# Two slots of their own for the gate inputs that are loaded back, and their first two loads ahead of the last two stores

## The chip, the cores and the metric

The kernel runs on one core of a Trainium2 chip. The metric is the device time of one execution in microseconds (us); with several runs it is their median. Times inside an execution are counted from the start of its profiled span.

## The reference, cut to what matters

Two layers follow each other, both with a residual sum: a graph layer (a gather of rows, scaled and summed by destination) and an LSTM whose hidden states are mixed into running sums.

```
support = layernorm(x) @ W.T + b                       # 6250 x 256
x = x + segment_sum(support[dst] * edge_weight, src)   # 100000 edges
z = layernorm(x)
xp = z @ W_ih.T + b_ih + b_hh                          # gate inputs, 6250 x 1024
for t in range(6250):                                  # one sequence
    i, f, g, o = split(xp[t] + h @ W_hh.T)
    c = sigmoid(f) * c + sigmoid(i) * tanh(g)
    h = sigmoid(o) * tanh(c)
w = argmax(h @ W_lin.T + b_lin) * h
out = x + 2 * h + prefix(w) * fw + suffix(w) * bw
```

## The kernel before, in words

The sequence of 6250 rows is cut into 125 segments of 50 rows. All segments are run side by side, as the 125 columns of one step. Each segment starts 64 steps early, so that its state has settled when its own rows begin: steps 0 to 63 run over rows that lie ahead of the segment, steps 64 to 113 over its own. The gate input of one row of every segment is one block of 128 partitions by 1016 values (508 KB). Each block is used two or three times.

The program has three long stages. First the edges are sorted into buckets, and the first portion of them is gathered and summed. In the second stage (about 755 to 1505 us) the edges of one row of every segment, a "place", are gathered in 12 tiles. GpSimd issues one indirect DMA for each tile (L522), TensorE multiplies the tile by a weighted one-hot matrix (L1539), and VectorE adds the product (L1046). Three places later the row is finished: it is normalised, projected to the gate input (L1558), and step u of the LSTM (L1565) runs straight from it. So steps 0 to 49 run beside the gather. The last place is 49, and step 49 runs after the last tile. In the third stage, from about 1518 us on, steps 50 to 113 run with no gather; their gate inputs are loaded back from HBM.

`take_input` (ScalarE, L640) writes the gate input of place j into slot q = j mod 2 of the tile `pr`. `seed_half` (L648) copies half of a slot into a PSUM bank as the start of the gate sums, and counts `seeded[x]`. `store_gate_input` (SyncE, L400) waits for `xe_r[1]`, stores the slot to `gate_input_scratch` and counts `st2[q]`. `load_gate_input` (L413) loads a block back into the same slot q of `pr` and counts `xp_l[q]`. ScalarE waits for that in `seed_loaded`, whose waits also hold the seed until the step before has read the bank.

Each engine works through its own instructions in order. SyncE issues the stores and the loads. A load into `pr` may go out only when the store that reads the same slot has landed and when the seeds that read it are done. In the program before, the order at the end of the second stage is store 48, load 50, store 49, load 51, and then a loop of loads from 52 on. On ScalarE the order is the rest of step 49 (its last operation is a tanh, L669), the two seeds of step 50, the two seeds of step 51, and then step 50. Step 50 on TensorE needs both seeds of step 50 and the hidden state of step 49.

Of the kernel before, what the change touches and what calls it, by code (L numbers as in the profile page):

```python
# [6 lines left out]
P = 128  # L7
# [5 lines left out]
SEGS, SEGL = 125, 50  # L13
# [28 lines left out]
LEAD = WARM - SEGL  # L42
LAG = 3
XW = SEGS + 2
XC = 8 * XW
# [12 lines left out]
def build(nc, A, out, slow_sweeps=SEGS, tol=TOL):  # L58
# [6 lines left out]
    ds = bass.ds  # L65
# [4 lines left out]
    xp_d = nc.dram_tensor("gate_input_scratch", [SEGL, P, XC], f32).ap()  # L70

    with ExitStack() as ctx:
        def sb(name, shape, dt=f32):
            return ctx.enter_context(nc.sbuf_tensor(name, shape, dt))
# [4 lines left out]
        def sem(name):  # L79
            return ctx.enter_context(nc.semaphore(name))  # L80
# [51 lines left out]
        pr = sb("pr", [P, 2, G4])  # L132
# [7 lines left out]
        flat_c = big_c[:].rearrange("p b f -> p (b f)")  # L140
# [3 lines left out]
        def at(home, first, rows, *dims, dt=f32):  # L144
            size = 1
            for n in dims:
                size *= n
            words = -(-size // 2) if dt == bf16 else size
            view = home[0:rows, first:first + words]
            if dt != f32:  # L150
                view = view.bitcast(dt)[:, 0:size]
            names = "abcde"[:len(dims)]
            spaced = " ".join(names)
            return view.rearrange(f"p ({spaced}) -> p {spaced}", **dict(zip(names, dims))) if len(dims) > 1 else view
# [58 lines left out]
        weighed = (w_even, w_odd)  # L213
        own = big_a[0:SEGS, :, :]
        x1 = big_b[0:SEGS, :, :]
        gate_in = [pr[:, q, 0:XC].rearrange("p (c k) -> p c k", c=8) for q in range(2)]


# [66 lines left out]
        st2 = [sem(f"gate_input_stored{i}") for i in range(2)]  # L285
        xp_l = [sem(f"gate_input_loaded{i}") for i in range(2)]
        bits = sem("gate_banks_written_once")
        small_t = sem("bias_and_logit_columns_in_psum")
        seeded = [sem(f"gates_seeded{x}") for x in range(2)]
# [48 lines left out]
        def _(sp):  # L338
# [35 lines left out]
            for g in range(-(-NB // STORED)):  # L374
                first, n = g * STORED, min(STORED, NB - g * STORED)
# [21 lines left out]
            def store_gate_input(j, l, q):  # L397
                sp.wait_ge(xe_r[1], j + 1)
                row = l if isinstance(l, int) else sp.snap(l)
                sp.dma_start(xp_d[ds(row, 1), :, :].rearrange("o p n -> p (o n)"), pr[:, q, 0:XC]).then_inc(st2[q], 16)  # L400
# [6 lines left out]
                    store_gate_input(it * 2 + q, it * 2 + (q - LEAD), q)  # L407

            def load_gate_input(u, l, q):
                for x in range(2):  # L410
                    sp.wait_ge(seeded[x], u - 1)
                row = l if isinstance(l, int) else sp.snap(l)
                sp.dma_start(pr[:, q, 0:XC], xp_d[ds(row, 1), :, :].rearrange("o p n -> p (o n)")).then_inc(xp_l[q], 16)  # L413

            for q in range(2):
                store_gate_input(SEGL - 2 + q, SEGL - 2 + q - LEAD, q)
                sp.wait_ge(st2[q], 16 * (SEGL // 2))
                load_gate_input(SEGL + q, SEGL - LEAD + q, q)
            with sp.Fori(SEGL // 2 + 1, WARM // 2) as it:
                for q in range(2):  # L420
                    load_gate_input(it * 2 + q, it * 2 + (q - LEAD), q)
            with sp.Fori(WARM // 2, STEPS // 2) as it:
                for q in range(2):
                    load_gate_input(it * 2 + q, it * 2 + (q - WARM), q)
# [139 lines left out]
        def _(act):  # L564
# [69 lines left out]
            def take_input(j, q, x, free=None):  # L634
                act.wait_ge(pj2[x], j + 1)
                if free is not None:
                    act.wait_ge(seeded[x], free)
                    act.wait_ge(st2[q], j * 8 - q * 8)
                for c in range(4):
                    ins = nc.scalar.activation(gate_in[q][:, 4 * x + c, 2:XW], bank[2 + x][:, c * SEGS:(c + 1) * SEGS],  # L640
                                               ACT.Identity, bias=bias[:, 4 * x + c:4 * x + c + 1])
                ins.then_inc(xe_r[x], 1)
# [1 line left out]
            def copy_input(j, q, first=False):  # L644
                copy_transposed(j, q, xt_p2, pj2[1], xt_r2, first, 2)

            def seed_half(q, x, w, b):
                nc.scalar.copy(bank[b + x][:, 0:4 * SEGS].rearrange("p (c k) -> p c k", c=4),  # L648
                               gate_in[q][:, 4 * x:4 * x + 4, w:w + SEGS]).then_inc(seeded[x], 1)

            def seed_loaded(u, pair, q, w, used=-1):
                act.wait_ge(xp_l[q], pair * 16 - (SEGL // 2 * 16 - 16))
                for x in range(2):
                    act.wait_ge(a_o[x], u + used)
                for x in range(2):
                    seed_half(q, x, w, 2 * q)

            def gates(u, q, x, far, b=None):
                g = bank[(2 * q if b is None else b) + x]
# [17 lines left out]
            def take_and_seed(u, q, w):  # L677
                for x in range(2):
                    take_input(u, q, x, None if isinstance(u, int) and u < 2 else u - 1)
                    act.wait_ge(xe_r[x], u + 1)  # L680
                    if not isinstance(u, int) or u > 0:
                        act.wait_ge(a_o[x], u)
                    seed_half(q, x, w, 0)

            def place(it, q, w=0, last=False):
                h = 2 * it + q if isinstance(it, int) else HALVES
                j, u = it * 2 + (q - LAG), it * 2 + (q - LAG - 1)
                if h > LAG + 1:
                    tanh_c(u - 1, 1 - q, 1)
                if h > 0 and not last:  # L690
                    act.wait_ge(prod, it * WIDE + (RING + TFROM[1] + q * PACE))
                    stage_gather(it * WIDE + (TFROM[1] + (q + 1) * PACE), 1 - q, PACE)
                if h > LAG:
                    take_and_seed(u, q, w)
                    for x in range(2):
                        gates(u, q, x, False, 0)
                    tanh_c(u, q, 0)
                if h >= LAG:
                    copy_input(j, 1 - q, h < LAG + 2)
# [16 lines left out]
            place(HALVES // 2, 0, 1, True)  # L716
            tanh_c(SEGL - 2, 0, 1)
            take_and_seed(SEGL - 1, 1, 1)
            step(SEGL - 1, 1, False, 0)
            seed_loaded(SEGL, SEGL // 2, 0, 1, 0)  # L720
            act.wait_ge(bits, 2)
            seed_loaded(SEGL + 1, SEGL // 2, 1, 1)
            with act.Fori(SEGL // 2, (WARM - 2) // 2) as it:
                for q in range(2):
                    step(it * 2 + q, q)
                    seed_loaded(it * 2 + (q + 2), it + 1, q, 1)
# [11 lines left out]
            with act.If(ok == 0):  # L738
# [6 lines left out]
                with act.Fori(0, slow_sweeps) as sweep:  # L745
# [4 lines left out]
                    with act.Fori(0, SEGL // 2 - 1) as it:  # L750
                        u, m = sweep * SEGL + it * 2 + STEPS, sweep * (SEGL // 2) + it + STEPS // 2
# [1004 lines left out]
```

## Time and profile before

| | us |
|---|---|
| median of three runs | 1850.2 |
| the three runs | 1849.69, 1850.2, 1853.89 |
| the profiled execution | 1853.58 |
| its span | 1851.8 |
| mean granted TensorE clock | 0.885 of full |
| TensorE busy | 1388.0 (75%) |
| VectorE busy | 1365.8 (74%) |
| GpSimd busy | 1204.2 (65%) |
| ScalarE busy | 543.2 (29%) |

The span lies between the first and the last instruction of the profiled execution; 1.8 us of its time lie around the span. The busy shares are averages over stages that have different limits, so they say little about a change at one point. What counts is what each engine waits for between about 1457 and 1523 us, where the last gathers, the last two stores and the first loads follow each other.

### The profile page before, as it was taken

What the parts mean: (1) busy time and instruction counts of PE and PEld (TensorE: products, weight loads), DVE (VectorE), ACT (ScalarE), POOL (GpSimd) and SP (SyncE); (2) the same over time, 40 slices, a digit from 0 to 9 for tenths busy, and PEclk for the clock granted to TensorE, in tenths of its full rate; (3) what the DMA queues carried; (4) which work ended last, traced back from release to release, by engine and by line L of the source; (5) the groups of instructions that cost most, each with busy time, mean ns of one, the idle gap of its engine ahead of it and who ended that gap; (6) DMA issues with size and microseconds to landing.
All of it is one profiled execution on the core that took longest, in us unless ns stands there. A gap on an engine that the chain in (4) does not pass through costs nothing.

```text
span 1851.8 us, 34357 instructions
## 1 busy us (share of the span) xinstructions
PE 1388.0 (75%) x8625; PEld 1154.8 (62%) x8625; DVE 1365.8 (74%) x4146; ACT 543.2 (29%) x1869; POOL 1204.2 (65%) x1275
## 2 busy tenths in 40 slices
PE   5587744554555458998988888889889878999991
PEld 2345533443444333787777777777777668899991
DVE  7979778888888955677777777777777644566665
ACT  1112200000000000333333333333333346666660
POOL 0304867777777757777777777777777700477772
PEclk9778967777777775899999999999999999999995
DMA  8101343333333643444444444444444763333334
GB/s 210 26 23 35 50 137 76 79 79 74 80 79 74 77 61 106 128 137 141 144 138 138 139 137 139 139 136 139 138 137 137 109 124 114 113 113 112 113 101 139
DMA packets 77430, 202.26 MB, mean 109 GB/s; under 512 B 28529, under 2 KB 30790, under 8 KB 76392
## 3 DMA queue, kind: packets, MB, share of 16 engines
q0 software_dynamic: 53808, 116.85, 27.3%
q1 hardware_dynamic: 23584, 84.98, 14.2%
q8 instruction: 15, 0.25, 0.1%
q14 instruction: 23, 0.19, 0.0%
HBM read 160.49 MB, written 41.10 MB: 109 GB/s over the span
## 4 chain that ended last, share of the span: by engine, by line
PE 27%; POOL 24%; DVE 22%; issue 17%; DVEq 3%; DMA 3%; ACT 3%; SPq 0%; POOLq 0%; ACTq 0%
POOL big_a L522 22%; PE bank L1565 10%; DVE big_a L975 7%; PE bank L1485 5%; PE bank L1539 5%; PE bank L1514 4%; PE bank L1558 1%; DVEq L1049 1%; DVE big_c L1166 1%; ACT big_c L669 1%; DVE big_c L1171 1%; DVE listed L914 1%; ACT bank L662 1%; DVE stats L893 1%; PE bank L1433 1%
## 5 line engine op out<-in xcount | busy, mean ns | idle before, releaser
L522 POOL DMA_INDIRECT big_a<-support_scratch,stg_g x636 | 608.3, 956 | 207.0 <-issue 192.3
L1539 PE MATMUL bank<-big_a,big_c 128*125 128x256 f32 x1272 | 412.3, 416 | 92.0 <-issue 51.0
L1565 PE MATMUL bank<-big_c 128*128 128x125 f32 x3648 | 457.2, 277 | 26.9 <-DVE big_c L1171 23.8
L1565 PEld LDWEIGHTS bank<-big_c 128*128 128x128 f32 x3648 | 446.7, 192 | 48.7 <-issue 36.0
L1046 DVE TENSOR_TENSOR big_b<-big_b,bank 125x256 f32 x881 | 366.5, 416 | 132.0 <-PE bank L1539 82.9
L1040 DVE TENSOR_SCALAR big_c<-consts_sb,listed 128x125 f32<-128x125 f32 x881 | 318.8, 362 | 73.4 <-PE bank L1539 62.1
L1539 PEld LDWEIGHTS bank<-big_a,big_c 128*125 128x125 f32 x1272 | 202.7, 197 | 179.2 <-DVE big_c L1040 113.1
L492 POOL DMA_INDIRECT big_a<-support_scratch,stg_g x245 | 236.2, 964 | 82.2 <-issue 69.2
L1485 PE MATMUL bank<-big_a 125*128 125x192 bf16 x800 | 119.5, 332 | 214.1 <-DVE big_a L975 214.1
L1485 PEld LDWEIGHTS bank<-big_a 125*128 125x128 bf16 x800 | 100.4, 132 | 237.5 <-DVE big_a L975 229.4
L1558 PEld LDWEIGHTS bank<-xt,w_ih 128*128 128x128 f32 x1600 | 213.3, 195 | 13.8 <-ACT xt L578 1.9
L1558 PE MATMUL bank<-xt,w_ih 128*128 128x125 f32 x1600 | 214.0, 278 | 1.7 <-ACT xt L578 1.7
L604 ACT CAST stg_g<-listed 128x12 uint32 (+4 forms) x84 | 15.8, 190 | 472.4 <-PE bank L1514 387.4
L669 ACT ACTIVATE big_c<-big_c 128x125 f32<-128x125 f32 x228 | 70.4, 309 | 233.5 <-DVE big_c L1166 233.5
L1514 PE MATMUL bank<-big_a,big_c 128*125 128x256 f32 x490 | 129.0, 414 | 11.6 <-DMA big_a<-support_scratch,stg_g 9.1
L640 ACT ACTIVATE pr<-bank,gate_bias 128x125 f32<-128x125 f32 x400 | 113.3, 367 | 75.1 <-PE bank L1558 74.4
L537 POOL TENSOR_TENSOR listed<-listed 125x256 f32<-125x256 f32 x50 | 36.5, 729 | 142.7 <-DVE listed L1295 142.5
L648 ACT COPY bank<-pr 128x500 f32<-128x500 f32 x228 | 126.6, 573 | 3.2
L975 DVE TENSOR_TENSOR big_a<-big_a,bank 125x3840 bf16<-125x3840 bf16 x30 | 124.3, 4142 | 0.0
L662 ACT ACTIVATE big_c<-bank 128x250 f32<-128x250 f32 x128 | 48.3, 378 | 241.7 <-PE bank L1565 241.7
L1514 PEld LDWEIGHTS bank<-big_a,big_c 128*125 128x125 f32 x490 | 94.6, 208 | 37.0 <-issue 12.9
L463 POOL DMA_INDIRECT record_scratch<-stg_r,stg_i x60 | 95.6, 1593 | 21.5 <-issue 16.8
(226 smaller groups left out, 1658.4 us busy)
## 6 DMA issues: line engine op xcount, KB each, us to landing
pr<-gate_input_scratch SPq DMA_DIRECT2D x64, 508.0 KB, 3.4
gate_input_scratch<-pr SPq DMA_DIRECT2D x50, 508.0 KB
big_a<-support_scratch,stg_g POOLq DMA_INDIRECT x881, 2.8
out<-big_a SPq DMA_DIRECT2D x5, 1120.0 KB
support_scratch<-pr SPq DMA_DIRECT2D x12, 448.0 KB
big_b<-in_x SPq DMA_DIRECT2D x2, 1904.0 KB
big_b<-in_x SPq DMA_DIRECT2D x1, 1792.0 KB
w_ih<-in_w_ih SPq DMA_DIRECT2D x1, 1024.0 KB
```

The source lines that it names most:

```text
L492: pool.indirect_dma_start(out=ring[:, s, :], out_offset=None, in_=sup_d, in_offset=bass.IndirectOffsetOnAxis(ap=stg_g[:, q, j:j + 1], axis ...
L522: pool.indirect_dma_start(out=ring[:, s, :], out_offset=None, in_=sup_d, in_offset=bass.IndirectOffsetOnAxis(ap=stg_g[:, q, n:n + 1], axis ...
L640: ins = nc.scalar.activation(gate_in[q][:, 4 * x + c, 2:XW], bank[2 + x][:, c * SEGS:(c + 1) * SEGS], ACT.Identity, bias=bias[:, 4 * x + c ...
L648: nc.scalar.copy(bank[b + x][:, 0:4 * SEGS].rearrange("p (c k) -> p c k", c=4), gate_in[q][:, 4 * x:4 * x + 4, w:w + SEGS]).then_inc(seede ...
L975: V.tensor_tensor(col_v[:, q].rearrange("p c k n e -> p (c k n e)"), col_h[:, q].rearrange("p c (o n) e -> p c o (n e)", o=1).broadcast_to ...
L1040: V.tensor_scalar(oneh[:, s % HOTS, 0:SEGS], iota[:, 0:SEGS], src_of[:, ds(t, 1)], w_of[:, ds(t, 1)], ALU.is_equal, ALU.mult).then_inc(oh_ ...
L1046: V.tensor_tensor(at, at, bank[4 + s % PSR][0:SEGS, 0:D], ALU.add).then_inc(added, 1)
L1485: ins = mm(bank[q][:, 0:6 * NPOS], slot_h[:, q, c // 2, :, c % 2], col_v[:, q, c // 2, :, :, c % 2].rearrange("p k n -> p (k n)"), start=c ...
L1514: mm(bank[4 + s % PSR][0:SEGS, 0:D], oneh[:, s % HOTS, 0:SEGS], ring[:, s % RING, :], start=True, stop=True).then_inc(prod, 1)
L1539: mm(bank[4 + s % PSR][0:SEGS, 0:D], oneh[:, s % HOTS, 0:SEGS], ring[:, s, :], start=True, stop=True).then_inc(prod, 1)
L1558: ins = mm(bank[2 + x][:, c * SEGS:(c + 1) * SEGS], w_ih[:, k, g:g + P], xt[:, q, k, 0:SEGS], start=k == 0, stop=k == 1)
L1565: return mm(bank[b + x][:, c * SEGS:(c + 1) * SEGS], w_hh[:, k, g:g + P], h_s[:, q, k, :], start=False, stop=True, skip_group_check=True)
```

## The change

There are two edits. First, the blocks that are loaded back no longer go into `pr`. They go into two slots of their own, `taken_in`, a part of the tile `big_c` that is free by then, and the seeds of steps 50 to 113 read them there. Second, SyncE's order at the end of the second stage is now load 50, load 51, store 48, store 49. The first two loads no longer wait for the seeds, since nothing has been in the new slots before. Load 50 waits for store 46 and load 51 for store 47. A wait for the stores 48 and 49 stands ahead of the loop of loads.

```
+        taken_in = [at(flat_c, 8192 + 1024 * q, P, 8, XW) for q in range(2)]
...
             def load_gate_input(u, l, q):
-                for x in range(2):
-                    sp.wait_ge(seeded[x], u - 1)
+                if not isinstance(u, int) or u >= SEGL + 2:
+                    for x in range(2):
+                        sp.wait_ge(seeded[x], u - 1)
                 row = l if isinstance(l, int) else sp.snap(l)
-                sp.dma_start(pr[:, q, 0:XC], xp_d[ds(row, 1), :, :].rearrange("o p n -> p (o n)")).then_inc(xp_l[q], 16)
-
+                sp.dma_start(taken_in[q].rearrange("p c k -> p (c k)"), xp_d[ds(row, 1), :, :].rearrange("o p n -> p (o n)")).then_inc(xp_l[q], 16)
+
+            for q in range(2):
+                sp.wait_ge(st2[q], 16 * (SEGL // 2 - 1))
+                load_gate_input(SEGL + q, SEGL - LEAD + q, q)
             for q in range(2):
                 store_gate_input(SEGL - 2 + q, SEGL - 2 + q - LEAD, q)
+            for q in range(2):
                 sp.wait_ge(st2[q], 16 * (SEGL // 2))
-                load_gate_input(SEGL + q, SEGL - LEAD + q, q)
...
-            def seed_half(q, x, w, b):
+            def seed_half(q, x, w, b, home):
                 nc.scalar.copy(bank[b + x][:, 0:4 * SEGS].rearrange("p (c k) -> p c k", c=4),
-                               gate_in[q][:, 4 * x:4 * x + 4, w:w + SEGS]).then_inc(seeded[x], 1)
+                               home[q][:, 4 * x:4 * x + 4, w:w + SEGS]).then_inc(seeded[x], 1)
...
-                    seed_half(q, x, w, 2 * q)
+                    seed_half(q, x, w, 2 * q, taken_in)
...
-                    seed_half(q, x, w, 0)
+                    seed_half(q, x, w, 0, gate_in)
```

On SyncE, this is the program before at the end of the second stage. The first two rows are the end of the loop that stores places 14 to 47; `gate_input_ready1` is `xe_r[1]`, `gate_input_stored0` is `st2[0]`.

```order
L405 REGISTER_ALU
L405 COMPARE_AND_BRANCH
L400 DMA gate_input_scratch<-pr 128x1016 [waits gate_input_ready1]
L413 DMA pr<-gate_input_scratch 128x1016 [waits gates_seeded1,gates_seeded0,gate_input_stored0]
L400 DMA gate_input_scratch<-pr 128x1016 [waits gate_input_ready1]
L413 DMA pr<-gate_input_scratch 128x1016 [waits gates_seeded1,gates_seeded0,gate_input_stored1]
L419 UNCONDITIONAL_BRANCH
```

The same place in the changed program:

```order
L406 REGISTER_ALU
L406 COMPARE_AND_BRANCH
L415 DMA big_c<-gate_input_scratch 128x1016 [waits gate_input_stored0]
L415 DMA big_c<-gate_input_scratch 128x1016 [waits gate_input_stored1]
L401 DMA gate_input_scratch<-pr 128x1016 [waits gate_input_ready1] x2
L424 UNCONDITIONAL_BRANCH [waits gate_input_stored1,gate_input_stored0]
```

The two loads stand right behind store 47, the last one of the loop, and the two last stores stand behind both loads.

On ScalarE, this is the end of step 49 and what follows it in the program before (`c_ready1` is the new cell state of the second half).

```order
L669 ACTIVATE big_c<-big_c 128x125 [waits c_ready1]
L648 COPY bank<-pr 128x500 [waits act_o_done1,act_o_done0,gate_input_loaded0]
L648 COPY bank<-pr 128x500
L648 COPY bank<-pr 128x500 [waits act_o_done0,act_o_done1,gate_input_loaded1,gate_banks_written_once]
L648 COPY bank<-pr 128x500
```

In the changed program:

```order
L674 ACTIVATE big_c<-big_c 128x125 [waits c_ready1]
L653 COPY bank<-big_c 128x500 [waits act_o_done1,act_o_done0,gate_input_loaded0]
L653 COPY bank<-big_c 128x500
L653 COPY bank<-big_c 128x500 [waits act_o_done0,act_o_done1,gate_input_loaded1,gate_banks_written_once]
L653 COPY bank<-big_c 128x500
```

Only the tile that the seeds read has another name; no instruction of ScalarE has moved, and none of TensorE, VectorE and GpSimd has.

## Rows read from the trace of the kernel before

**Rows 1.** The chain of waits from 1505 to 1524 us: start, length, what.

```profile
1506.09 3.85 PE bank L1558 x32
...
1511.12 2.66 DMA gate_input_scratch<-pr
1513.78 0.01 issue
1513.80 3.55 DMA pr<-gate_input_scratch
1517.35 0.03 ACTq L654
1517.38 0.51 ACT bank L648
1517.89 0.59 issue
1518.48 2.48 PE bank L1565 x20
```

**Rows 2.** Instructions of ScalarE in order of time, 1513 to 1519.6 us: start, length, what.

```profile
1517.09 0.31 ACT L669 ACTIVATE big_c<-big_c 128x125 f32<-128x125 f32 x1 [0.55 <-DVE big_c L1166]
1517.31 2.09 ACT L648 COPY bank<-pr 128x500 f32<-128x500 f32 x4
```

**Rows 3.** All engines in order of time, 1518 to 1545 us: step 51.

```profile
1520.98 0.38 ACT L662 ACTIVATE big_c<-bank 128x250 f32<-128x250 f32 x1 [1.58 <-PE bank L1565]
...
1523.69 0.31 ACT L669 ACTIVATE big_c<-big_c 128x125 f32<-128x125 f32 x1 [0.55 <-DVE big_c L1166]
1523.91 1.07 ACT L648 COPY bank<-pr 128x500 f32<-128x500 f32 x2
...
1525.57 0.38 ACT L662 ACTIVATE big_c<-bank 128x250 f32<-128x250 f32 x1 [0.59 <-PE bank L1565]
```

**Rows 4.** All engines, 1490 to 1518 us: SyncE's DMA issues.

```profile
1497.63 0.34 SPq L400 DMA_DIRECT2D gate_input_scratch<-pr  x1
...
1505.88 0.35 SPq L413 DMA_DIRECT2D pr<-gate_input_scratch  x1
```

**Rows 5.** SyncE alone, 1455 to 1480 us: the issue of store 47.

```profile
1475.19 0.33 SPq L400 DMA_DIRECT2D gate_input_scratch<-pr  x1
```

**Rows 6.** Busy time by stretch: stretch, its length, then PE, PEld, DVE, ACT, POOL, granted clock, DMA share, GB/s.

```profile
1420.00:1440.00 20.00, 18.09 (x122) 15.69 (x121) 14.64 (x66) 8.51 (x28) 15.13 (x17) 1.00 0.47 137
...
1460.00:1475.00 15.00, 11.79 (x60) 9.24 (x60) 8.19 (x33) 4.53 (x16) 11.36 (x12) 0.90 0.96 74
...
1485.00:1495.00 10.00, 7.57 (x36) 6.56 (x35) 4.87 (x19) 1.83 (x7) 1.89 (x2) 0.66 0.95 119
```

**Rows 7.** DMA from 1460 to 1475 us: queue, packets, MB, share; then issues with median us to landing.

```profile
q0 software_dynamic: 402, 1.11, 95.5%
...
big_a<-support_scratch,stg_g POOLq DMA_INDIRECT x12, 12.4
```

**Rows 8.** The same from 1475 to 1490 us.

```profile
q0 software_dynamic: 407, 1.10, 89.1%
q1 hardware_dynamic: 142, 0.52, 8.4%
...
big_a<-support_scratch,stg_g POOLq DMA_INDIRECT x10, 15.1
```

**Rows 9.** DMA from 1484 to 1485 us: the first packets of store 47.

```profile
q1 hardware_dynamic: 3, 0.01, 3.0%
```

**Rows 10.** DMA from 1503 to 1504 us: the first packets of store 48.

```profile
q1 hardware_dynamic: 24, 0.10, 23.7%
```

**Rows 11.** TensorE in order of time, 1500 to 1519 us: the last tiles of the gather.

```profile
1500.71 0.67 PE L1539 MATMUL bank<-big_a,big_c 128*125 128x256 f32 x2 [0.30 <-issue]
...
1502.54 0.67 PE L1539 MATMUL bank<-big_a,big_c 128*125 128x256 f32 x2 [0.27 <-issue]
...
1504.02 1.29 PE L1539 MATMUL bank<-big_a,big_c 128*125 128x256 f32 x4
```

**Rows 12.** Eight products at half and at full clock, chain of waits from 1400 us.

```profile
1461.06 1.70 PE bank L1565 x8
...
1476.27 0.89 PE bank L1565 x8
```

**Rows 13.** The seeds between 1500 and 1560 us: ns min/median/max.

```profile
L648 ACT COPY bank<-pr x22: 565/569/580, 1509.3 to 1556.6; 128x500 f32<-128x500 f32 x22
```

## The prediction

> **What bounds the kernel now.** I read the chain of waits around the end of the gather first, since it names the transfers that the change moves. It runs over store 49 (2.66 us) and load 51 (3.55 us) into a seed and from there into step 50 [rows 1]. Taken at its word, 2.66 + 3.55 = 6.21 us of DMA stand on the path and would go. So I read ScalarE in order of time next, to see what the seed itself waited for. Its four seed copies start at 1517.31 and end at 1519.40, with no gap, 0.22 us after the start of the last tanh of step 49 (1517.09) [rows 2]. In the settled third stage, where loads are long there, the seeds also start 0.22 us behind that tanh: 1523.69 and 1523.91 [rows 3]. The first copy even starts 0.04 us ahead of the landing of load 51, at 1513.80 + 3.55 = 1517.35. It needs only load 50, which was issued at 1505.88 [rows 4]; with the 3.55 us of load 51 that one landed by about 1509.4. The four copies take 2.09 us, so the third, the first one that needs load 51, starts at about 1517.31 + 2.09 / 2 = 1518.3, almost 1 us after the landing. The chain joins a wait in ScalarE's queue to the copy that is running there; it is not what held it.
>
> Third, I read what the DMA does where the loads will go. From 1457 us on, GpSimd still issues a tile every 1.25 us (12 in 15 us), but the DMA is 96% busy at only 74 GB/s, against 47% at 137 GB/s before [rows 6]. Landing takes 12.4 us and then 15.1 us [rows 7, 8]. The last tiles run on TensorE 1.83 us apart (1500.71, 1502.54) with gaps of 0.3 us [rows 11], and a tile of 128 KB at 74 GB/s takes 1.77 us. Between 1460 and 1505 us the gather transfers therefore set the pace, and step 49 and all that follows begin when the last tile has landed.
>
> **The change part by part.** *The loads leave the stretch of 1505 to 1517 us.* Two transfers and SyncE's wait for store 49 go from there. The next in line is what already holds the seeds: the tanh of step 49, in ScalarE's order. Step 50 starts at 1518.48, 0.1 us after the second copy ends (1517.31 + 2.09 / 2 + the overlap of 0.06 = 1518.4). If load 51 had landed long before, no copy would start earlier. Gain: 0, and at most the 0.04 us by which first copy and landing cross.
>
> *Load 50 goes into the slow gathers.* SyncE issued store 47 at 1475.19 [rows 5]. Load 50 now follows at once, near 1475.6, since store 46 is a whole place older. That is in the middle of the backlog. Store 47, issued at 1475.19, moved its first packets only after 1484 [rows 9], and store 48, issued at 1497.63, only after 1503 [rows 4, 10], when the gathers were done. So a transfer of this queue is served about when the gathers issued just before it are, and load 50 will move right behind store 47, at about 1487 to 1491 us, ahead of the nine or ten tiles issued after it. What does that cost those tiles? Store 47 shows it. In the 15 us with its 0.52 MB the gathers moved 1.10 MB, in the 15 us without it 1.11 MB [rows 7, 8]. The difference of 0.01 MB at 0.074 MB per us is 0.14 us. The slow tiles are limited by something that leaves the engines room. That is the lower end. The upper end is the full time that such a block takes from all 16 engines, 8.4% of 15 us = 1.26 us [rows 8]. I take 0.4 us, near the lower end, because the nearest row is a block of the same size at the same place, and a little above it, since load 50 comes directly behind that block and the gathers get no turn in between. It goes to the end in full: the last tile lands later, and so does all the rest. Nothing can be gained here, since nothing is taken away ahead of the last tile.
>
> *Load 51* waits for store 47, whose packets all lie before 1490 us [rows 8], and is issued then. By the pattern of store 48 it is served behind the last gather (GpSimd issues only two after 1485 [rows 6]), at about 1504 us. It moves in under 3 us and is needed at about 1518.3, so over 10 us remain. Cost: 0. *Stores 48 and 49* stand behind it in SyncE's order. They are issued when their gate inputs are ready, as before, and move up to 1.3 us later than they did, because load 51 is ahead of store 48. Their rows, 34 and 35 of each segment, are read only by steps 98 and 99.
>
> Here the Trainium skill speaks against the change more than the trace does. DMA: Bandwidth & Descriptors, section "Queues, rings and completion order", has each DMA engine go round among the queues with work, a packet at a time. By that rule load 51 would be served within the backlog, from 1490 us on, and would take its turn from the last tiles too. The 9 us of store 47 and the 6 us of store 48 ahead of their first packets do not agree with it [rows 4, 5, 9, 10].
>
> *The new wait ahead of the loop of loads.* Store 49 is issued at 1511.12 and landed at 1513.78 [rows 1]; the first load of the loop needs the seeds of step 50 and cannot go out before about 1518.4. Some 4.6 us cover the wait. Behind it stand all later loads, and if the cover were gone, load 52 would be late, which is needed only at 1523.9.
>
> *The seeds read another tile.* 128 copies of 569 ns change their source. I take no difference. The spread of one is 565 to 580 ns [rows 13], so the ends are -0.5 and +1.4 us of ScalarE's time over all, and after the two seeds of a step ScalarE still idles 0.59 us until the gate sums come [rows 3], which hides either. The loads land in another part of the same memory; for that I have no row that shows a difference, and take none.
>
> *Sum.* 1853.58 + 0.4 = 1854.0 against the profiled execution's own time. That execution lies 3.4 us above the median of 1850.2, near the slowest of the three runs (1853.89); the other two are 1849.69 and 1850.2. The effect of 0.4 us is carried to the median: 1850.6. Since runs without any change fall at 1850 and at 1854, a median of few runs can fall at either.
>
> **The rivals.** *A: the chain of waits is right.* Store 49 and load 51 hold the seeds of step 50, and 6.2 us go: 1850.2 - 6.2 = 1844.0. For it speaks the chain itself, and that landing and first copy fall within 0.04 us [rows 1, 2]. Against it: the copy needs another load, starts before the landing, and keeps the usual distance of 0.22 us from the tanh. Even with the loads gone, that tanh ends at 1517.40.
>
> *B: the queues share within the backlog, and the clock falls.* Both loads are served ahead of the last tiles, for 2 x 1.26 = 2.5 us in full. TensorE stands idle for as long, near 1490 to 1500 us, and its granted clock falls to the lower level (1.2 GHz), as it did between 1485 and 1495 (mean 0.66) after gaps in its work [rows 6]. There eight products take 1.70 us in place of 0.89 [rows 12]. Today this falls among the tiles, and TensorE catches up, because the tiles set the pace. If it falls on the projection of place 49, 3.85 us at full clock [rows 1], it costs 3.85 x (1.70 / 0.89 - 1) = 3.5 us that nothing hides. Sum: 6.0 us, 1856.2. It decides against the change from 5.6 us on, so both parts are needed; with load 50 alone at its upper end and the clock as now it is 1851.5, no change. For it: the clock has fallen twice in this stretch. Against it: the 1.10 against 1.11 MB, and the late packets of both stores. This is also the outcome that the rule quoted above would lead to.
>
> *C: the change does nothing at all,* because load 50 too is served behind the last gather: 1850.2.
>
> **How the numbers follow.** A measurement of this kernel can tell about 0.3%, 5.6 us, from no change. My forecast (load 50 costs 0.1 to 1.3 us, nothing is gained) has 0.66, C 0.20, A 0.06, B 0.08. Forecast and C give "within 0.3%": 0.86, and A and B the other two sides. Range: the forecast's own 1850.3 to 1851.5, widened by what runs of one kernel differ: down to 1847.5, which takes in a small part of A, and up to 1855.0, which takes in a median at the upper of the two levels.
>
> **What would show it.** In the changed profile load 50 is issued near 1475.6 and load 51 near 1490. The seeds of step 50 still start 0.22 us behind the last tanh of step 49, and the chain no longer names a DMA between 1511 and 1517 us. The distance from the end of the last tile to the start of step 50 on TensorE (1518.48 - 1505.31 = 13.2 us) stays the same, and the last tile is up to 1.3 us later. I am wrong if that distance shrinks by more than 0.3 us, if the last tile moves by more than 1.3 us, or if the settled steps of the third stage, 4.59 us each (1520.98 to 1525.57 [rows 3]), change their length.

## The result, and the profile after

| | median us | lowest to highest | runs |
|---|---|---|---|
| before | 1852.84 | 1847.23 to 1856.02 | 22 |
| changed | 1857.14 | 1851.34 to 1863.64 | 22 |

The ratio is 1.0026, with a 95% interval from 1.0016 to 1.0036: about 4.8 us slower, and at least 3.0 (the medians are 4.3 us apart). That is clear of the runs' spread, but inside the 0.3% that I had called no change. The time lies 2.1 us above the upper end of my range. With so many runs each, a difference much smaller than 5.6 us can be told.

The profiled executions hide it. The kernel before was caught at 1853.58, in the upper third of its runs, and the changed kernel at 1853.52, the fourth shortest of its 22; the spans are 1851.8 and 1851.7 us. So spans can't be compared here. What can be compared is a distance inside each execution, from one event that the change doesn't touch to another behind it. I take the issue of store 47 as the start, the projection of place 49 (L1558 before, L1563 now), which follows the last tile, and the first product of step 50.

These are the DMA issues of SyncE in the changed kernel, in order of time (start, length from the first start to the last end of the row, what); store 47 first, then the two loads (the second starts at 1489.52), then store 48 and store 49:

```profile
1473.45 0.33 SPq L401 DMA_DIRECT2D gate_input_scratch<-pr  x1
1474.00 15.86 SPq L415 DMA_DIRECT2D big_c<-gate_input_scratch  x2
1494.23 18.61 SPq L401 DMA_DIRECT2D gate_input_scratch<-pr  x2
```

And TensorE of the same execution from 1500 us on, to be read beside [rows 11] and [rows 1]:

```profile
1501.55 1.05 PE L1570 MATMUL bank<-big_c 128*128 128x125 f32 x8
1503.79 1.28 PE L1544 MATMUL bank<-big_a,big_c 128*125 128x256 f32 x4 [1.19 <-issue]
1504.90 0.38 PE L1552 MATMUL bank<-consts_sb,xn 125*128 125x125 f32 x2
1505.86 5.43 PE L1563 MATMUL bank<-xt,w_ih 128*128 128x125 f32 x32 [0.58 <-ACT xt L583]
1513.17 3.81 PE L1570 MATMUL bank<-big_c 128*128 128x125 f32 x32 [1.88 <-issue]
```

Two things are new. TensorE stands still for 1.19 us ahead of the last two tiles, where it had no gap before. And the projection takes 5.43 us in place of 3.84, because the granted clock is at its lower level for the first 3 us of it. This is the stretch from 1506 to 1509 us (PE, PEld, DVE, ACT, POOL, granted clock, DMA share, GB/s); from 1509 to 1511 the clock was 0.94:

```profile
1506.00:1509.00 3.00, 3.00 (x14) 3.00 (x15) 0.86 (x4) 0.31 (x1) 0.00 (x0) 0.50 0.03 7
```

From store 47 to the projection it is 1505.86 - 1473.45 = 32.4 us; before it was 1506.09 - 1475.19 = 30.9.

What the DMA does in that gap is seen in single microseconds. From 1501 to 1502 us, from 1502 to 1503, and from 1503 to 1504 (queue, packets, MB, share of the 16 engines):

```profile
q0 software_dynamic: 22, 0.05, 49.0%
q1 hardware_dynamic: 39, 0.16, 44.2%
```

```profile
q1 hardware_dynamic: 43, 0.16, 52.2%
q0 software_dynamic: 4, 0.00, 0.2%
```

```profile
q1 hardware_dynamic: 90, 0.33, 79.6%
q0 software_dynamic: 17, 0.04, 14.5%
```

Queue q1 is SyncE's, q0 carries the gathers. The block that starts to move at 1501 is load 51, issued at 1489.52, since load 50 had landed by then. GpSimd had issued its last tile at 1484.51, so load 51 overtakes it: 0.32 MB of the block move from 1501 to 1503 us, the gathers all but stop in the second of these microseconds, and their last 0.04 MB move at 1503. Before, the first packets of store 48 came at 1503, with the last 0.07 MB of the gathers, about half a tile [rows 10].

The seeds of step 50 are where they were, right behind the last tanh of step 49 (ScalarE in order of time, changed kernel):

```profile
1518.45 0.31 ACT L674 ACTIVATE big_c<-big_c 128x125 f32<-128x125 f32 x1 [0.55 <-DVE big_c L1171]
1518.66 2.09 ACT L653 COPY bank<-big_c 128x500 f32<-128x500 f32 x4
```

That is 0.21 us behind the start of the tanh, against 0.22 us in [rows 2]. No DMA holds them, now or before. The chain of waits names no DMA between 1511 and 1517 us any more, and a settled step still takes 4.59 us (1522.34 to 1526.93). Two of the signs that the prediction named went the other way: the distance from the end of the last tile to the start of step 50 is 1519.84 - 1505.07 = 14.8 us in place of 13.2, the 1.6 us of the slower projection, and the last tile, counted from store 47, ends 31.6 us later in place of 30.1, which is 1.5 us and not at most 1.3.

### The profile page after: what moved, and what is told of

Same layout as the page of the kernel before. It is cut to its first block, busy times and chain, and to the rows that moved or that the text cites. A ratio compares the mean times of both kernels' runs of the same rounds, so it can differ in the third digit from the quotient of the medians.

```text
span 1851.7 us, 34356 instructions
## 1 busy us (share of the span) xinstructions
PE 1388.2 (75%) x8625; PEld 1154.9 (62%) x8625; DVE 1367.0 (74%) x4146; ACT 542.7 (29%) x1869; POOL 1204.4 (65%) x1275
## 3 DMA queue, kind: packets, MB, share of 16 engines
q0 software_dynamic: 53808, 116.85, 26.9%
## 4 chain that ended last, share of the span: by engine, by line
PE 29%; DVE 22%; POOL 22%; issue 17%; DVEq 3%; DMA 3%; ACT 3%; SPq 0%; POOLq 0%; ACTq 0%
POOL big_a L527 20%; PE bank L1570 10%; DVE big_a L980 7%; PE bank L1544 6%; PE bank L1490 5%; PE bank L1519 4%; PE bank L1563 2%; DVEq L1054 2%; POOL record_scratch L468 1%; DVE big_c L1171 1%; DMA record_scratch<-stg_r,where_b 1%; ACT big_c L674 1%; DVE big_c L1176 1%; DVE big_b L1051 1%; DVE listed L919 1%
## 5 line engine op out<-in xcount | busy, mean ns | idle before, releaser
L1563 PEld LDWEIGHTS bank<-xt,w_ih 128*128 128x128 f32 x1600 | 215.1, 196 | 12.7 <-ACT xt L583 1.5
L1563 PE MATMUL bank<-xt,w_ih 128*128 128x125 f32 x1600 | 215.5, 279 | 0.8 <-ACT xt L583 0.8
L974 DVE TENSOR_TENSOR big_a<-bank,slot_iota 125x2560 bf16<-125x2560 f32 x30 | 84.5, 2818 | 0.0
```

Of the source, the lines that this page charges most:

```text
L1563: ins = mm(bank[2 + x][:, c * SEGS:(c + 1) * SEGS], w_ih[:, k, g:g + P], xt[:, q, k, 0:SEGS], start=k == 0, stop=k == 1)
```

## The experiments

**Two lengths of one program.** In thirteen of the eighteen runs the kernel before took 2383 to 2412 us in place of 1853. One and the same chip showed both on different occasions (before 1854.2 us and 2411.6 us), so it isn't a property of a chip. Where it takes about 2400 us, TensorE is held up in the whole gather stage. The line of the steps' weight loads in the profile of slots_only there (engine, line, waited for: us, times, longest):

```profile
PEld bank L1567 <- issue: 299.3, 285, 3.3
```

Before, the same row reads 36.0 us in 64 times. I don't know what it waits for; the profile names nothing. GpSimd then waits for the staging of its indices (524.8 us, against 14.7 before), the last tiles come 1.33 us apart on TensorE and so aren't paced by the transfers, and no order of the loads differs from the kernel before. These runs are told here, but only those at about 1853 us can tell the theories apart. The last four runs took about 2400 us as well, so what they were meant to settle is partly open.

The cuts below show an edit against the changed kernel, for spread_before against the kernel before. Lines with + are added; most of the lines that they replace are left out.

Theory at this point: one of the two loads, or both, move among the slow gathers (backlog theory). Rivals: the new slots themselves cost time; and rival A of the prediction, by which something is gained where loads come early.

**The slots alone.** Own slots, with the old order:

```
             for q in range(2):
+                store_gate_input(SEGL - 2 + q, SEGL - 2 + q - LEAD, q)
+                sp.wait_ge(st2[q], 16 * (SEGL // 2))
                 load_gate_input(SEGL + q, SEGL - LEAD + q, q)
```

> Own slots, but the old order: store 48, load 50, store 49, load 51. Backlog theory (the loss comes from the block that is moved among the slow gathers): no load lies among them, so 1852.8 us, the time of before, within 1.5 us. If the new slots themselves cost time (another part of the memory): 1857, as the changed kernel. Rival A of the prediction: nothing gained here either, since store 49 still precedes load 51.

Measured: 2400.6 us, against about 2402 for the kernel before, ratio 0.9994 (0.9983 to 1.0004).

> Own slots, old order (store 48, load 50, store 49, load 51), where before takes about 1853 us. Backlog theory: ratio 1.000 within 0.001, since no load lies among the slow gathers. If the slots cost the time: 1.0026.

Measured: 1852.75 us, ratio 1.0003 (0.9993 to 1.0013). The slots cost nothing.

**Both loads early.** The loads 50 and 51 stand right behind the loop that stores places 0 to 13; their rows, 36 and 37, are places 0 and 1, and stored by then.

```
+            for q in range(2):
+                sp.wait_ge(st2[q], 16 * (LEAD // 2))
+                load_gate_input(SEGL + q, SEGL - LEAD + q, q)
             with sp.Fori(LEAD // 2, SEGL // 2 - 1) as it:
```

> Own slots, both loads issued at place 14, where the DMA is under half busy, long before the slow gathers. Backlog theory: 1852.8 us, as before, within 1.5 us. Rival A (the chain of waits is right, store 49 and load 51 hold step 50): 1846.6, 6.2 us faster than before.

> Both loads at place 14, ahead of the slow gathers. Backlog theory: ratio 1.000 against before, within 0.001, at about 1853 us. Rival A (the chain of waits is right): 0.9967, 6.2 us faster.

> On the two chips tried so far the kernel before took 2402 us, and no version differed from it. Where it takes about 1853 us: backlog theory: ratio 1.000 within 0.001, since both loads move at place 14, ahead of the slow gathers. Rival A (the chain of waits is right): 0.9967. If the slots themselves cost the time: 1.0026.

Measured at about 2400, 2400 and 2380 us: 1.0004 (0.9993 to 1.0014), 0.9998 (0.9987 to 1.0008) and 0.9993 (0.998 to 1.0006).

> Both loads at place 14, where before takes about 1853 us. Backlog theory: ratio 1.000 within 0.001. Rival A (store 49 and load 51 hold step 50): 0.9967. If the slots cost the time: 1.0026.

Measured: 1851.33 us, ratio 0.9997 (0.9986 to 1.0007). The loss is gone, and the 6.2 us of rival A (0.9967) are excluded. Here both loads were issued at about 952 us and had landed hundreds of microseconds before, and still ScalarE shows the same picture as [rows 2]:

```profile
1513.32 0.31 ACT L675 ACTIVATE big_c<-big_c 128x125 f32<-128x125 f32 x1 [0.54 <-DVE big_c L1172]
1513.53 2.09 ACT L654 COPY bank<-big_c 128x500 f32<-128x500 f32 x4
```

The chain of waits now runs over the tanh, and over no DMA:

```profile
1513.32 0.04 ACT big_c L675
...
1513.54 0.57 ACT bank L654
1514.11 0.59 issue
1514.70 1.35 PE bank L1571 x10
```

So the 6.2 us of DMA in the chain of [rows 1] were a wrong link, as its order of start and landing had said.

**The two loads apart.** Load 50 alone ahead, load 51 behind both stores:

```
+            sp.wait_ge(st2[0], 16 * (SEGL // 2 - 1))
+            load_gate_input(SEGL, SEGL - LEAD, 0)
             for q in range(2):
                 store_gate_input(SEGL - 2 + q, SEGL - 2 + q - LEAD, q)
...
+            load_gate_input(SEGL + 1, SEGL - LEAD + 1, 1)
```

> Only load 50 ahead of the last two stores; load 51 behind both. Backlog theory with load 50 alone as the cost: 1856 to 1857, as the changed kernel, and the last tile about 1.3 us later, counted from the issue of store 47, than before. If load 51 is the costly one, because it takes turns with the last gathers: 1853 to 1854.

> The first look at this kernel fell on a chip on which the kernel before takes 2402 us: there TensorE is held up at every step of the gather stage, the last gathers do not set the pace, and no version differed. On a chip on which it takes about 1853 us. Backlog theory with load 50 alone as the cost: a ratio of 1.0015 to 1.0026, as the changed kernel. If load 51 is the costly one: 1.000 to 1.001.

Measured at about 2400 us: 0.9995 (0.9986 to 1.0005) and 0.9996 (0.9985 to 1.0007).

> Only load 50 ahead of the last stores, where before takes about 1853 us. If load 50 alone is the cost: 1.0015 to 1.0026. If load 51, which takes turns with the last gathers, is the larger part: 1.000 to 1.001.

Measured: 1852.27 us, ratio 1.0000 (0.9991 to 1.001). Load 50 was issued at 1479.19, and GpSimd issued nine more tiles after it.

Load 51 alone ahead, as soon as store 47 has landed; load 50 behind store 48:

```
+            sp.wait_ge(st2[1], 16 * (SEGL // 2 - 1))
+            load_gate_input(SEGL + 1, SEGL - LEAD + 1, 1)
+            store_gate_input(SEGL - 2, SEGL - 2 - LEAD, 0)
+            sp.wait_ge(st2[0], 16 * (SEGL // 2))
+            load_gate_input(SEGL, SEGL - LEAD, 0)
+            store_gate_input(SEGL - 1, SEGL - 1 - LEAD, 1)
```

> Only load 51 ahead, issued when store 47 has landed; load 50 waits for store 48. If a transfer is served in the order of issue, load 51 moves behind the last gather and costs nothing: 1852.8. If it takes turns with the last gathers, 2 to 3 us of the 4.3 are here: 1855 to 1856.

> On a chip where before takes about 1853 us. Served in the order of issue, load 51 costs nothing: ratio 1.000. If it takes turns with the last gathers (in the changed profile some packets of load 51 move ahead of the last packets of the last gather): 1.001 to 1.002.

Measured at about 2400 us: 0.9998 (0.9989 to 1.0006) and 0.9993 (0.9982 to 1.0004).

> Only load 51 ahead, issued when store 47 has landed, where before takes about 1853 us. Served strictly in the order of issue: 1.000. If it takes turns with the last gathers: 1.001 to 1.002.

Measured: 1856.83 us, ratio 1.0026 (1.0015 to 1.0037), on the same chip as load50_ahead_3 and against the same 31 runs of the kernel before. Load 51 alone brings the whole loss, load 50 alone none that these runs can tell. In its profile, TensorE in order of time shows the last tiles stretched, with gaps of 0.94 and 1.24 us:

```profile
1501.19 0.67 PE L1544 MATMUL bank<-big_a,big_c 128*125 128x256 f32 x2
1501.70 1.05 PE L1570 MATMUL bank<-big_c 128*128 128x125 f32 x8
1503.69 0.67 PE L1544 MATMUL bank<-big_a,big_c 128*125 128x256 f32 x2 [0.94 <-issue]
1504.19 1.05 PE L1570 MATMUL bank<-big_c 128*128 128x125 f32 x8
1506.48 1.10 PE L1544 MATMUL bank<-big_a,big_c 128*125 128x256 f32 x4 [1.24 <-issue]
```

The same tiles in load50_ahead_3 have no gap, though store 47 and load 50 moved among the gathers between 1486 and 1499 us. In these 13 us the gathers moved 0.86 MB (0.066 MB per us), and in the 7 us behind them 0.59 MB (0.084), so part of the delay was made up:

```profile
1503.71 0.67 PE L1544 MATMUL bank<-big_a,big_c 128*125 128x256 f32 x2
1504.21 1.05 PE L1570 MATMUL bank<-big_c 128*128 128x125 f32 x8
1505.24 0.67 PE L1544 MATMUL bank<-big_a,big_c 128*125 128x256 f32 x2
1505.74 1.05 PE L1570 MATMUL bank<-big_c 128*128 128x125 f32 x8
1506.70 1.45 PE L1544 MATMUL bank<-big_a,big_c 128*125 128x256 f32 x4
```

**The changed kernel again.**

> The changed kernel itself. Where the kernel before takes about 1853 us: ratio 1.0026, as in the result. Where it takes about 2400 us, as on the three chips tried so far: backlog theory: 1.000, since there the last tiles are not set by the gather transfers; if the new slots or the order cost time by themselves: 1.002, 4 to 5 us, on any chip.

Measured: 1858.0 us against 1854.2, ratio 1.0027 (1.0014 to 1.0039). The loss is there on this chip as well. TensorE in this profile shows the same stop, larger:

```profile
1504.64 1.95 PE L1544 MATMUL bank<-big_a,big_c 128*125 128x256 f32 x4 [1.49 <-issue]
1507.47 5.77 PE L1563 MATMUL bank<-xt,w_ih 128*128 128x125 f32 x32 [0.46 <-ACT xt L583]
1515.12 3.81 PE L1570 MATMUL bank<-big_c 128*128 128x125 f32 x32 [1.88 <-issue]
```

The seven profiles at about 1853 us, side by side (us; 32 products take 3.8 us at full clock, as in [rows 1]):

| kernel | store 47 issued | projection starts | distance | projection | step 49's products |
|---|---|---|---|---|---|
| before | 1475.19 | 1506.09 | 30.9 | 3.84 | 3.81 |
| slots_only_3 | 1471.99 | 1500.42 | 28.4 | 3.84 | 3.81 |
| loads_early_4 | 1471.70 | 1500.88 | 29.2 | 3.83 | 5.43 |
| load50_ahead_3 | 1478.64 | 1508.82 | 30.2 | 3.84 | 3.81 |
| changed | 1473.45 | 1505.86 | 32.4 | 5.43 | 3.81 |
| after_again | 1472.93 | 1507.47 | 34.5 | 5.77 | 3.81 |
| load51_ahead_3 | 1476.53 | 1508.55 | 32.0 | 3.84 | 5.44 |

With load 51 behind the stores, or early, the mean distance is (30.9 + 28.4 + 29.2 + 30.2) / 4 = 29.7 us; with load 51 at the landing of store 47 it is (32.4 + 34.5 + 32.0) / 3 = 33.0. The difference is 3.3 us, and no value of one group lies in the other. Counted from the last tile that GpSimd issues, it comes out about the same: 19.8, 18.4, 18.5 and 19.1 us against 21.4, 24.0 and 21.0, a difference of 3.1. The clock fell to its lower level within the 64 products behind the last tile in all three of the second group (1.6, 1.9 and 1.6 us) and in one of four of the first (1.6 us): 1.7 - 0.4 = 1.3 us. Together 4.6 us, against 4.8 us by the ratio. From store 47 to the first product of step 50 the means are 42.4 and 47.1 us, 4.7 apart. These are single executions, so the split into 3.3 and 1.3 is rough, and in after_again the clock is low from 1505 us on, so that some of its cost lies in the first part. That the longer gap makes the clock fall isn't shown: in loads_early_4 it fell as well, at 1508 us, with no gap over 0.31 us ahead of any of the last four tiles.

**Both at once, behind store 47.** This was to tell the place of issue from the number of blocks: load 51 waits for store 45 and goes out right behind load 50.

```
-                sp.wait_ge(st2[q], 16 * (SEGL // 2 - 1))
+                sp.wait_ge(st2[q], 16 * (SEGL // 2 - 2))
```

> The changed kernel, but load 51 waits for store 45 in place of store 47, so that it is issued right behind load 50, about 12 to 15 us earlier. Theory (a block costs only where it is served among the last gathers, when nothing can be caught up): ratio 1.000 to 1.001, though three blocks now move in the backlog. Rival (each further block in the backlog costs its own time): 1.0026 or more.

Measured: 2411.6 us, with the kernel before at 2411.55, ratio 1.0000 (0.999 to 1.001). There no order of the loads makes a difference, so it doesn't tell.

**The cause of the slow gathers.** The places of the last tiles that hold no edge have weight 0 and row 0. The edit gives them rows 0, 48, 96 and so on, by partition (`spread_row` is 48 times the number of the partition):

```
-                V.tensor_copy(row_of[:, a:a + T], pack_i[:, 0:T]).then_inc(unpacked, 1)
+                link(V.tensor_scalar(src_of[:, a:a + T], w_of[:, a:a + T], 0.0, spread_row[:], ALU.is_equal, ALU.mult))
+                V.tensor_tensor(row_of[:, a:a + T], pack_i[:, 0:T], src_of[:, a:a + T], ALU.add).then_inc(unpacked, 1)
+                dve.wait_ge(unpacked, p + 1)
```

> The changed kernel, but the empty places of the tiles (weight 0) gather rows spread over the table in place of row 0 all of them. If the slow gathers come from many reads of one row, the DMA share falls to about half in the last 45 us of the gather, the backlog is gone, and the last tiles come every 1.3 us in place of 1.8: about 25 tiles x 0.5 = 12 us faster, and some more at the end of the first portion, 1838 to 1845; load 50 then costs nothing. If the slowness has another cause, 1857 as the changed kernel, plus 1 to 2 us for the two added operations.

> The changed kernel with the empty places of the tiles (weight 0) gathering rows 0, 48, 96 and so on by partition in place of row 0 all of them; two more operations on VectorE in each unpacking. If reads of one row make the last gathers slow: GpSimd's pace of 1.25 us is then the limit, the last tile comes 10 to 14 us earlier, two to four us go for the added operations: 1840 to 1846, and the same as spread_before within 1 us. If not: 1859.

> The same edit of the gathered rows in the kernel before. One-row theory: 1840 to 1846, a ratio of 0.994 to 0.997. Otherwise 1854.

> The same edit with own slots and both loads at place 14. One-row theory: as spread_before, 1840 to 1846, within 1 us: with the backlog gone the place of the loads no longer matters. If rival A is right after all (store 49 and load 51 on the path), it is 4 to 6 us faster than spread_before.

Measured, all at about 2400 us: 0.9999 (0.9987 to 1.001), 1.0011 (1.0001 to 1.0021), 1.0009 (1.0 to 1.0019) and 1.0008 (0.9999 to 1.0017). The times don't test the gain; if anything, the two added operations show, with 0.1%. But the transfers answer the question. From 1990 to 2050 us, the end of the gather stage in both, this is both_at_once, with row 0 in the empty places:

```profile
q0 software_dynamic: 1365, 3.76, 55.6%
```

and this is spread_before:

```profile
q0 software_dynamic: 1344, 3.67, 19.8%
```

Nearly the same bytes take 20% of the engines' time in place of 56%. From 1900 to 1960 us, ahead of the last tiles, the two hardly differ (19.0% for 3.20 MB, 21.2% for 3.67 MB). Over the whole execution it is 18.3% in place of 20.5%, for the same 53808 packets. So the slowness of the last gathers comes from the reads of row 0 in the empty places. This was seen where the kernel takes about 2400 us. Whether the version gains where the transfers set the pace wasn't seen, and no version here beat the kernel before; loads_early_4 equals it.

## Why the prediction was wrong, point by point

**Where the seeds are held: right.** The gain from taking 6.2 us of DMA out of the chain was put at 0, and loads_early_4 shows 0. The order of starts and landings on the engine told more than the chain's link.

**Load 50 among the slow gathers: right in kind.** I took 0.4 us, between 0.1 and 1.3; load50_ahead_3 shows a ratio of 1.0000 with an interval from -1.7 to +1.9 us. Its block did move among the gathers, and the last tiles came without a gap. The estimate from store 47, 1.10 against 1.11 MB [rows 7, 8], was too low for the stretch itself: 0.066 in place of 0.074 MB per us over 13 us is 0.1 MB, by my estimate 1.4 us for the two blocks. Part of that was made up behind them, and what is left can't be told from 0.

**Load 51: this is the step that failed.** The prediction said that by the pattern of store 48 it is served behind the last gather, cost 0. It cost all of the loss. I took the pattern from the wrong neighbour. Store 48 was issued at 1497.63 and its first packets came 6 us later, when half a tile was left. Load 51 was issued at 1489.52 in the changed profile, when more of the backlog was outstanding, and its first packets came at 1501, 12 us later, with 0.09 MB of the last tile's 0.13 still to move (about one tile in after_again and load51_ahead_3). Store 47 had shown that this is possible: the tiles issued around it needed 15.1 us to land [rows 8] (so did the one issued at 1475.02, just ahead of it, which landed at 1490), but its own packets began after 9 us [rows 5, 9], and 0.34 MB of its 0.52 had moved by 1487. So it had overtaken tiles issued before it. Both numbers, 15.1 and 9, were in my rows. I read the 9 us as "about in the order of issue" and didn't set them beside the 15.1. The rule of the Trainium skill that I quoted (DMA: Bandwidth & Descriptors, "Queues, rings and completion order", engines go round among the queues with work) forecast rightly that load 51 is served ahead of gathers issued before it. The traces agree only in part: its first packets come late, 10 to 13 us after the issue in three profiles. Why they come that late, no run shows.

**The price of a block.** I put the full price at 1.26 us, the block's own time on 16 engines. At the end of the backlog it was about 3.3 us. In load51_ahead_3 the last tiles come 2.5 and 2.8 us apart in place of 1.8, so 1.7 us of it are seen at two tiles. In the changed profile the gathers move almost nothing from 1502 to 1503 us, while the block moves 0.16 MB with the engines 52% busy. The last tile stood still while the engines, on average, were half idle. The rest of the 3.3 us I can't place.

**The clock.** Rival B had named it, with 3.5 us, for a lower level through the whole projection. It fell for a part of it, 1.6 to 1.9 us. The mechanism that I held least likely but for A, with a chance of 0.08, was the one that happened, with load 51 as its only carrier. That its sum of 6.0 us lies near the 4.8 measured is partly luck: its two terms, 2.5 and 3.5 us, were 3.3 and 1.3 as measured above.

**The range.** The time before, 1850.2, was the median of three runs, and 22 runs gave 1852.84. That alone moves the forecast by 2.6 us. I had taken the three runs for two levels, 1850 and 1854, and set the upper end to hold both, but not a loss on top of them; the 22 runs lie between 1847.23 and 1856.02.

## What to carry to other kernels

A transfer that is issued early isn't free because its data is needed late: ask whose transfers it will be served among, and whether those still have work behind them in which a delay can be caught up. The same 508 KB cost nothing that could be measured when they were issued with nine tiles still to be issued (load 50), and 4 to 5 us when they were issued after the last one and moved ahead of its last packets (load 51). To place such a load, go back to where the DMA is half idle; here that was possible from the fourteenth place on (engines 43% to 57% busy around 950 us), and it was neutral. And where the chain of waits names a transfer, look whether the instruction behind it starts before the landing, and what its distance to its own engine's last instruction is elsewhere.

## What the runs showed of the hardware

- The last gathers, with row 0 of HBM in their empty places, took 56% of the DMA engines' time in both_at_once; with the empty places spread over many rows nearly the same bytes took 20% in spread_before.
- A block of SyncE's queue moved its first packets 5 to 6 us after the issue with three to four tiles of the gather outstanding (store 48 in before and slots_only_3), and 7 to 13 us with about seven or more (store 47 and load 51 in all profiles at about 1853 us). Load 51 overtook the last tile, issued 3 to 7 us before it, though it did not alternate with the gathers from the start.
- The issue of load 50 right behind store 47, whose packets hadn't begun to move, held SyncE for 2.13, 2.64 and 2.27 us (changed, after_again, load50_ahead_3), against 0.34 us for load 51, issued in the same backlog once store 47 had landed.
- The same program ran at 1853 us and at 2400 us at different times, also on one chip. At 2400 us the granted clock was 0.79 in place of 0.89 over the span, and TensorE's waits put down to issue were eight times as long in the steps' line. The cause isn't known.
